# One TensorE program of attention and an FP4 feed-forward: Gram products in six pieces, the small chain's steps at other places, own matrices for the last batch, and a short end for three engines

## The chip, the core and the metric

The kernel runs on one core of one Trainium2 chip. The core has five engines with programs of their own: TensorE (PE; its weight loads are shown as PEld), VectorE (DVE), ScalarE (ACT), GpSimd (POOL) and SyncE (SP), which issues all DMAs here. They are tied by semaphores. The metric is the time of one execution in microseconds (us), the median of several runs. The profile comes from one profiled execution; its span starts when the first engine starts and ends with the last instruction.

## What is computed

`x` is (4, 2048, 256) float32: four batches of 2048 tokens. It is normalised row by row. Then two branches work on the result `xn`, and their product is added to `x`:

```python
xn = layernorm(x)
# attention, linear: no softmax, the norms run over the 2048 tokens
Q, K, V = xn @ Wq.T + bq, xn @ Wk.T + bk, xn @ Wv.T + bv
Q, K = l2_norm_over_tokens(Q), l2_norm_over_tokens(K)
tailor = 1.0 / (256 + einsum('bnc,bc->bn', Q.T, K.sum(-1) + 1e-6))
matrix = einsum('bmn,bcn->bmc', K, V)
s = xn + gamma * (V.sum(-1) + einsum('bnm,bmc->bcn', Q, matrix)) * tailor
# feed-forward, inputs and weights of each product rounded to blocks of FP4
h = silu(fp4(xn) @ fp4(w_gate).T) * (fp4(xn) @ fp4(w_up).T)      # 704 wide
g = silu(fp4(h) @ fp4(w_down).T)
out = x + s * g
```

## The kernel before

**Tiling.** The 8192 rows are taken in 32 pairs of 128-row tiles, 8 pairs to a batch. The kernel is one software pipeline over pairs, written once as `iteration(p, k, b, i)` for each engine and driven by `drive` (L290): iterations -1 to 11 written out, a hardware loop over batches 1 and 2 whose body is eight iterations, then iterations 28 to 32 written out, and a tail of iterations 33 to 43. In iteration p the input of pair p+3 is normalised and its scales found, pair p+1 is transposed, pair p goes through the gate and up products, pair p-1 is rounded to FP4, pair p-2 goes through the down product, pair p-10 through the attention product, and pair p-12 is added to `x` and stored. An iteration has two halves, j = 0 and 1 (one tile each), and each half two chunks c of 352 of the 704 hidden columns.

**The heavy work of an iteration.** On PE, for each chunk, `gate_up` (12 matmuls of 352 columns into `GU`), and with it a piece of the attention product of an older pair, `s_half` (6 matmuls of 128 columns, `GU<-Mx,xnT`); for each half the transposes of the rounded hidden values (`TR<-id,hq`, 11), those of the next inputs, and `down_product` (17 matmuls of 256 columns into `DS`). ACT makes `sil` from a gate chunk, copies transposes out of PSUM (`hqT`, `xqT`, `xnT`) and makes `gring` from `DS`. DVE multiplies `sil` with the up chunk (`h`, L840), finds the block scales (`ham`, `hss`, `hrr`), rounds (`ht`, L877, and `hg`, L880, which need `hT` of ACT, which needs `ht` of POOL, which needs `hrr`), scales (`hq`, four of 704), and makes `y` from the attention product and `gring` (`e_half`, `e_mul`). POOL divides by the scales and adds `y` and `x` (`o`, L527; L522 for the last seven pairs). `gate_up` may write a chunk once `h` of the chunk before last is done.

**The chain.** Q, K and V aren't formed. For each batch the products of the normalised rows with themselves, the Gram matrix, are summed over the 16 tiles of the batch in one PSUM bank `G` (L1389: 16 matmuls of 512 columns for its first block row, "gram0", and 16 of 384 for the second, "gram1"). From it a chain of small steps between PE (`ask`), ACT (`copy`), POOL (`inv`) and DVE (`answer`), all through the one bank `G`, makes the matrix `Mx` and a factor `unm` by which the rows of that batch are multiplied: turn, t1q, t1k, squares, norms, raw, tailor, product, top, high_low. The last, L974 to L980, writes `unm` and `Mx`, and `s_half` of the batch's first pair waits for it. Before it writes, DVE waits until `y` of all earlier batches is done, since there is one `Mx` and one `unm`.

**What sets the order.** Each engine runs its program in order. Where a chain step stands is a table with keys (i, j, slot): i is the iteration within the batch (i = p - 8b - 5), j the half, and slot 0, 1 or 2 a place in the half: on PE slot 0 is after the hidden transposes, slot 1 after the row transposes, slot 2 after the down product. ASKS is PE's table, ANSWERS DVE's, COPIES ACT's; the last batch has tables of its own (..._END), since its chain has no later iteration to spread into. For batches 0 to 2 the new matrices are first used at i = 5, j = 1. For the last batch this is iteration 34, in the tail, where PE only multiplies rows by `Mx` (`s_product`, 12 matmuls of 256 columns for a pair, into four places of `GU` in turn).

## Time and profile before

| | us |
|---|---|
| three runs | 630.25, 631.48, 631.04 (median 631.04) |
| the profiled execution, whole | 630.21 |
| its span | 628.4 |
| PE busy | 556.2 (89%) |
| DVE busy | 565.3 (90%) |
| ACT busy | 411.0 (65%) |
| POOL busy | 240.6 (38%) |

The profiled execution is 0.83 us under the median, and 1.8 us of it lie outside the span. The shares are means over stages in which different engines set the pace. PE's busy time is of pipelined matmuls whose ends are modelled, so a full PE row says that PE was never without work, not how fast it was. Where an engine waits, the row of the waiting instruction has the idle time and what ended it in brackets. A row by stretch has, behind the stretch and its length, the busy time and instruction count of PE, PEld, DVE, ACT and POOL, then the clock granted to TensorE (1.00 is 2.4 GHz, 0.50 is 1.2 GHz), the DMA share and GB/s.

### The profile page before, as it was taken

To read this page: it belongs to the slowest core of one execution; us is meant where nothing else is said; L and a number is where in the kernel's file an instruction comes from. 1 tells how busy PE (TensorE), PEld (TensorE's weight loads), DVE (VectorE), ACT (ScalarE), POOL (GpSimd) and SP (SyncE) were. 2 spreads that over 40 slices of the span, in tenths; PEclk is the share of its full clock that TensorE was granted. 3 is DMA by queue.
4 is the path that set the end of the run, shared out by engine and by line. 5 is a ranking of instruction groups with operands and counts; after the bars stand their busy time and mean duration, and the time that the engine had idled before them with its cause. 6 is when DMAs were issued, how large, how long until landed. Compare 5 with 4: busy or idle time off the path is not lost.

```text
span 628.4 us, 15141 instructions
## 1 busy us (share of the span) xinstructions
PE 556.2 (89%) x4957; PEld 427.8 (68%) x4957; DVE 565.3 (90%) x1201; ACT 411.0 (65%) x884; POOL 240.6 (38%) x208
## 2 busy tenths in 40 slices
PE   0276889999999999999999888999999999999667
PEld 0253667677787777678787665778888676788555
DVE  6979899999989999999899997999999999976824
ACT  3475788767678777667677775767777776555320
POOL 4443143443323344434443342443533344223316
PEclk9967899999999999999999999999999999999898
DMA  7010000000001001111101111111101111141213
GB/s 238 17 35 17 18 19 18 18 18 19 19 32 37 18 2 52 52 53 52 52 2 52 52 56 52 51 53 51 28 26 52 52 35 34 37 152 34 67 49 137
DMA packets 17473, 29.15 MB, mean 46 GB/s; under 512 B 2672, under 2 KB 4848, under 8 KB 17392
## 3 DMA queue, kind: packets, MB, share of 16 engines
q1 hardware_dynamic: 17392, 28.13, 13.7%
q8 instruction: 44, 0.72, 0.5%
q14 instruction: 37, 0.30, 0.2%
HBM read 19.73 MB, written 8.39 MB: 45 GB/s over the span
## 4 chain that ended last, share of the span: by engine, by line
PE 41%; DVE 34%; issue 15%; ACT 4%; POOL 2%; DVEq 2%; DMA 1%; POOLq 0%; SPq 0%; ACTq 0%
PE GU L1322 17%; PE DS L1332 5%; DVE hg L880 4%; DVE hq L888 4%; DVE h L840 4%; PE G L1389 4%; DVE ham L847 3%; PE DS L1334 3%; PE TR L1284 3%; DVE y L899 2%; DVE xq L829 2%; PE GU L1342 2%; DVE xt L820 2%; DVE st L794 1%; DVE xam L804 1%
## 5 line engine op out<-in xcount | busy, mean ns | idle before, releaser
L1322 PE MATMUL GU<-wgu,xqT 128*128 128x352 f16 x1536 | 255.8, 317 | 11.0 <-DVE h L840 4.3
L1322 PEld LDWEIGHTS GU<-wgu,xqT 128*128 128x128 f16 x1536 | 148.7, 100 | 88.4 <-issue 8.7
L592 ACT ACTIVATE sil<-GU,wkap 128x352 f32<-128x352 f32 x128 | 70.8, 553 | 71.6 <-PE GU L1322 70.5
L515 POOL TENSOR_TENSOR ht<-h,hrr 128x1408 f32<-128x1408 f32 x32 | 82.9, 2589 | 84.1 <-DVE hrr L854 82.5
L1332 PE MATMUL DS<-wdT,hqT 128*128 128x256 f16 x704 | 88.5, 275 | 2.6 <-ACT hqT L599 2.6
L840 DVE SCALAR_TENSOR_TENSOR h<-GU,wkap,sil 128x352 f32<-128x352 f32 x128 | 69.4, 542 | 18.8 <-ACT sil L592 15.6
L888 DVE TENSOR_TENSOR hq<-hg,hs 128x704 f16<-128x704 f16 x128 | 77.0, 642 | 1.0
L471 POOL TENSOR_TENSOR rs<-ve,half 128x2 f32<-128x2 f32 x32 | 25.2, 787 | 136.2 <-DVE ht L877 122.3
L481 POOL TENSOR_TENSOR xnat<-xs,xnat 128x510 f16<-128x510 f32 (+1 forms) x32 | 37.0, 1156 | 99.5 <-DVE hq L888 94.4
L1332 PEld LDWEIGHTS DS<-wdT,hqT 128*128 128x128 f16 x704 | 66.9, 99 | 11.7 <-ACT hqT L599 2.9
L1342 PE MATMUL GU<-Mx,xnT 128*128 128x128 f16 (+1 forms) x648 | 59.9, 233 | 5.2 <-DVE Mx L980 4.5
L1342 PEld LDWEIGHTS GU<-Mx,xnT 128*128 (+1 forms) x648 | 49.3, 99 | 17.6 <-issue 6.2
L628 ACT ACTIVATE gring<-DS,hun 128x256 f32<-128x256 f32 (+1 forms) x64 | 29.9, 467 | 43.6 <-issue 30.3
L599 ACT COPY hqT<-TR 128x768 f16<-128x768 f16 x64 | 51.0, 797 | 7.5 <-PE TR L1284 6.5
L877 DVE SCALAR_TENSOR_TENSOR ht<-hT,ht 128x1408 f32<-128x1408 f32 x32 | 51.8, 1618 | 3.5 <-ACT hT L641 3.4
L1284 PE MATMUL TR<-id,hq 128*128 128x128 f16 x704 | 49.7, 219 | 4.1 <-DVE hq L888 3.8
L1334 PE MATMUL DS<-wdT,hqT 128*128 128x256 f16 x384 | 52.6, 273 | 0.0
L880 DVE SCALAR_TENSOR_TENSOR hg<-hT,ht 128x1408 f16<-128x1408 f32 x32 | 51.7, 1616 | 0.0
L847 DVE TENSOR_REDUCE ham<-h 128x88 f32<-128x1408 f32 x32 | 51.4, 1607 | 0.0
L488 POOL TENSOR_TENSOR xt<-xs,xrr 128x512 f32<-128x512 f32 x32 | 34.1, 1066 | 36.1 <-DVE hq L888 28.4
L1284 PEld LDWEIGHTS TR<-id,hq 128*128 128x128 f16 x704 | 42.7, 98 | 6.8 <-DVE hq L888 5.1
L641 ACT ACTIVATE hT<-ht 128x1408 f32<-128x1408 f32 x32 | 43.9, 1371 | 2.8 <-POOL ht L515 2.2
(152 smaller groups left out, 932.7 us busy)
## 6 DMA issues: line engine op xcount, KB each, us to landing
xin<-in_L_attn_x SPq DMA_DIRECT2D x34, 256.0 KB, 2.9
xe<-in_L_attn_x SPq DMA_DIRECT2D x25, 256.0 KB, 2.8
out<-o SPq DMA_DIRECT2D x25, 256.0 KB, 2.1
algebra<-in_L_ffn_w_down SPq DMA_DIRECT2D x1, 704.0 KB, 6.4
gring<-in_L_ffn_w_gate SPq DMA_DIRECT2D x1, 640.0 KB, 4.6
gring<-in_L_ffn_w_up SPq DMA_DIRECT2D x1, 640.0 KB, 5.2
xs<-in_L_attn_x SPq DMA_DIRECT2D x2, 256.0 KB, 4.5
xt<-in_L_attn_x SPq DMA_DIRECT2D x2, 256.0 KB, 5.1
```

What stands on the lines that cost most here:

```text
L515: g.tensor_tensor(paired(ht[:, 0:2 * I]), paired(h[:, q]), spread(hrr[:, q], 4 * CB), ALU.mult).then_inc(S["ht_d"], 1)
L592: a.activation(sil[:, c], GU[:, c, 0, 0:CH], ACT.Silu, scale=wkap[:, 0:1]).then_inc(S["sil_d"], 1)
L840: v.scalar_tensor_tensor(h[:, k, (2 * j + c) * CH:(2 * j + c + 1) * CH], GU[:, c, 1, 0:CH], wkap[:, 0:1], sil[:, c], ALU.mult, ALU.mult).t ...
L847: v.tensor_reduce(per_block(ham[:, :]), paired_in_order(h[:, q]), AX.X, ALU.max, apply_absolute_value=True).then_inc(S["ham_d"], 1)
L877: v.scalar_tensor_tensor(ht[:, 0:2 * I], hT[:, 0:2 * I], CUT, ht[:, 0:2 * I], ALU.max, ALU.subtract).then_inc(S["hw_d"], 1)
L880: v.scalar_tensor_tensor(hg[:, 0:2 * I], hT[:, 0:2 * I], CUT, ht[:, 0:2 * I], ALU.max, ALU.subtract).then_inc(S["hg_d"], 1)
L888: v.tensor_tensor(paired(hq[:, q, j, at:at + I]), paired(hg[:, j * I:(j + 1) * I]), spread(scales[:, q, j * HB:(j + 1) * HB], HB), ALU.mul ...
L1284: last = t.transpose(TR[:, bank, zz * P:(zz + 1) * P], hq[:, q, j, z * P:(z + 1) * P], id16[:, :])
L1322: last = t.matmul(GU[:, c, m, 0:CH], xqT[:, k, j, 2 * a_ + kc], wgu[:, b_, kc, 2 * m + c], start=(z == 0 and kc == 0), stop=(z == 2 and kc ...
L1332: t.matmul(DS[:, 0:D], hqT[:, j, z], wdT[:, z], start=(z == 0), stop=False)
L1334: last = t.matmul(DS[:, 0:D], hqT[:, j, LOCH + z], wdT[:, NCH + z], start=False, stop=(z == LOCH))
L1342: last = t.matmul(bank, slot[:, j, 2 * a_ + kc], Mx[:, b_, kc, columns], start=(i == 0 and kc == 0), stop=(i == 2 and kc == KD - 1))
```

## The change

It has four parts.

- **Gram products in six pieces.** gram0 is now four asks of four tiles (it was two of eight), gram1 two of eight tiles (it was one of sixteen). The first piece of gram0 moves into the end of the batch before (i = 6), where it belongs to batch b + 1.
- **The chain's other steps for batches 0 to 2** move later by up to four slots, and `inv` on POOL moves from the end of i = 2 to i = 3. For the last batch high_low moves earlier: PE's transposes by one slot, DVE's part from the end of iteration 33 to the middle of 32.
- **Own matrices for the last batch.** `Mx_end` and a second column of `unm` are written and read by batch 3, and its high_low no longer waits for `y` of the earlier batches.
- **A short end.** Behind iteration 32, PE, ACT and DVE run a `tail()` of their own in place of iterations 33 to 43. SP and POOL keep theirs.

```diff
         ASKS = {(-3, 0, 2): "weights_q", (-3, 1, 2): "weights_k", (-2, 0, 2): "weights_v",
-                (-1, 1, 2): "gram0_first", (0, 0, 1): "gram0_last", (0, 1, 2): "gram1", (1, 0, 2): "turn", (1, 1, 2): "t1q",
-                (2, 0, 1): "t1k", (2, 1, 0): "norms", (2, 1, 2): "raw", (3, 0, 2): "tailor", (3, 1, 2): "product",
-                (4, 1, 0): "top", (5, 0, 0): "high_low"}
-        ANSWERS = {(-4, 1, 1): "own_basis", (0, 1, 0): "gram0", (1, 0, 1): "gram1", (1, 1, 0): "turn", (2, 0, 2): "squares",
-                   (2, 1, 1): "norms", (3, 1, 0): "tailor", (4, 0, 1): "product", (4, 1, 1): "top",
-                   (5, 0, 1): "high_low"}
+                (-2, 1, 2): "gram0_0", (-1, 0, 1): "gram0_1", (-1, 1, 1): "gram0_2", (6, 1, 2): "gram0_0", (0, 0, 1): "gram0_3",
+                (0, 1, 2): "gram1_0", (1, 0, 0): "gram1_1", (1, 0, 2): "turn", (2, 0, 0): "t1q", (2, 0, 2): "t1k",
+                (2, 1, 2): "norms", (3, 0, 2): "raw", (3, 1, 2): "tailor", (4, 0, 2): "product", (4, 1, 2): "top",
+                (5, 0, 1): "high_low"}
+        ANSWERS = {(-4, 1, 1): "own_basis", (0, 1, 0): "gram0", (1, 0, 1): "gram1", (1, 1, 0): "turn", (2, 1, 0): "squares",
+                   (3, 0, 0): "norms", (4, 0, 0): "tailor", (4, 1, 0): "product", (5, 0, 0): "top", (5, 0, 2): "high_low"}
...
-                    (3, 0, 2): "top", (3, 1, 1): "high_low"}
+                    (3, 0, 2): "top", (3, 1, 0): "high_low"}
...
-                       (2, 0, 1): "norms", (2, 1, 2): "tailor", (3, 0, 1): "product", (3, 1, 0): "top", (4, 1, 2): "high_low"}
+                       (2, 0, 1): "norms", (3, 0, 0): "tailor", (3, 0, 1): "product", (3, 0, 2): "top", (3, 0, 3): "high_low"}
...
-                    if step == "high_low":
+                    if step == "high_low" and not (isinstance(b, int) and b == BATCHES - 1):
 
                         wait(dve, "y_d", 4 * b * PB)
...
+            def tail():
+                for p in range(PAIRS + 1, PAIRS + LAGE):
+                    for j in range(2):
+                        e_mul(p, p % 2, j)
...
+            def tail():
+                last = BATCHES - 1
...
+                p, k, first = PAIRS + 1, (PAIRS + 1) % 2, PAIRS + 1 - LAGE
+                s_pair(first)
+                for c in range(2):
+                    hidden_transposes(p, k, 0, c, False)
+                s_pair(first + 1)
+                for c in range(2):
+                    hidden_transposes(p, k, 1, c, False)
+                down_product(p, k, 0)
+                s_pair(first + 2)
+                down_product(p, k, 1)
+                for e in range(first + 3, PAIRS):
+                    s_pair(e)
```

The two `tail()` shown are VectorE's and TensorE's. ScalarE's holds `hidden_out` and `g_out` for the two tiles of pair 31, one tile after the other. In COPIES, t1q moves from (2, 0, 0) to (2, 0, 1) and raw from (3, 0, 1) to (3, 1, 0). `hidden_out` is the two `hqT` copies of a tile, `g_out` its `gring`, and `s_pair(e)` the attention product of pair e; `first` is pair 23, and pairs from 24 on belong to the last batch.

**TensorE from iteration 32 to the end.** `G<-mtop,ones` is the ask of top, `G<-id,mt` that of high_low. Before:

```order
L1342 MATMUL GU<-Mx,xnT 128x256 x6
L1448 MATMUL G<-mtop,ones 128x1
L1284 MATMUL TR<-id,hq 128x128 x11
L1453 MATMUL G<-id,mt 128x128 x4
L1332 MATMUL DS<-wdT,hqT 128x256 x11
L1334 MATMUL DS<-wdT,hqT 128x256 x6
L1342 MATMUL GU<-Mx,xnT 128x256 x6
L1284 MATMUL TR<-id,hq 128x128 x11
L1332 MATMUL DS<-wdT,hqT 128x256 x11
L1334 MATMUL DS<-wdT,hqT 128x256 x6
...
L1342 MATMUL GU<-Mx,xnT 128x256 x102
```

After:

```order
L1478 MATMUL G<-id,mt 128x128 x4
L1354 MATMUL DS<-wdT,hqT 128x256 x11
L1356 MATMUL DS<-wdT,hqT 128x256 x6
L1365 MATMUL GU<-Mx,xnT 128x256 x18
L1306 MATMUL TR<-id,hq 128x128 x11
L1365 MATMUL GU<-Mx_end,xnT 128x256 x12
L1306 MATMUL TR<-id,hq 128x128 x11
L1354 MATMUL DS<-wdT,hqT 128x256 x11
L1356 MATMUL DS<-wdT,hqT 128x256 x6
L1365 MATMUL GU<-Mx_end,xnT 128x256 x12
L1354 MATMUL DS<-wdT,hqT 128x256 x11
L1356 MATMUL DS<-wdT,hqT 128x256 x6
```

Rows of the attention product now stand between the transposes of pair 31 and its down products, and 72 matmuls are left behind them instead of 96.

**VectorE over the same stretch**, from `y` of the first tile of pair 22 on (`ktop` to `kap` is top, `unm` to `Mx` is high_low). Before:

```order
L911 SCALAR_TENSOR_TENSOR y<-GU,unm,gring 128x256
L870 SCALAR_TENSOR_TENSOR hs<-hss,hbq,hs 128x44 x2
L877 SCALAR_TENSOR_TENSOR ht<-hT,ht 128x1408
L880 SCALAR_TENSOR_TENSOR hg<-hT,ht 128x1408
L969 COPY ktop<-G 128x1
L970 RECIPROCAL kap<-G 128x1
L972 TENSOR_SCALAR kap<-kap 128x1
L888 TENSOR_TENSOR hq<-hg,hs 128x704 x4
L911 SCALAR_TENSOR_TENSOR y<-GU,unm,gring 128x256 x3
L974 TENSOR_SCALAR unm<-ktop 128x1
L978 TENSOR_SCALAR Mx<-G,kap 128x512
L980 SCALAR_TENSOR_TENSOR Mx<-G,kap,Mx 128x512
```

After:

```order
L983 COPY ktop<-G 128x1
L984 RECIPROCAL kap<-G 128x1
L986 TENSOR_SCALAR kap<-kap 128x1
L884 SCALAR_TENSOR_TENSOR hs<-hss,hbq,hs 128x44 x2
L891 SCALAR_TENSOR_TENSOR ht<-hT,ht 128x1408
L990 TENSOR_SCALAR unm<-ktop 128x1
L994 TENSOR_SCALAR Mx_end<-G,kap 128x512
L996 SCALAR_TENSOR_TENSOR Mx_end<-G,kap,Mx_end 128x512
L894 SCALAR_TENSOR_TENSOR hg<-hT,ht 128x1408
L902 TENSOR_TENSOR hq<-hg,hs 128x704 x4
L925 SCALAR_TENSOR_TENSOR y<-GU,unm,gring 128x256 x19
```

Top moved ahead of `hs` and `ht`, high_low ahead of `hg`, and the other 19 `y` now stand in a row.

**VectorE in the loop, iteration i = 2 to 4** keeps its rows; squares (L931, L934) move behind `hg` of i = 2, norms to the start of i = 3, and tailor from behind `hg` of i = 3 to the start of i = 4.

## Rows read from the trace of the kernel before

**Rows 1.** Busy time by stretch: the last batch's first five iterations, and the end

```profile
511.10:583.60 72.50, 71.59 (x651) 55.62 (x648) 62.27 (x120) 40.81 (x81) 21.29 (x14) 1.00 0.17 56
583.60:628.40 44.80, 29.64 (x242) 24.46 (x241) 22.00 (x51) 9.34 (x17) 17.70 (x13) 0.86 0.25 89
```

**Rows 2.** DVE's waits in batch 1's chain, 270 to 330: total us, times, longest

```profile
DVE h L840 <- ACT sil L592: 2.2, 3, 0.9
DVE ht L877 <- ACT hT L641: 0.5, 1, 0.5
```

**Rows 3.** The same in batch 0's chain, 150 to 190

```profile
DVE h L840 <- ACT sil L592: 1.4, 3, 0.7
DVE ht L877 <- ACT hT L641: 0.8, 1, 0.8
```

**Rows 4.** Timeline of PE: gram1 of batch 1; first use of `Mx` of batch 1

```profile
265.27 3.61 PE L1389 MATMUL G<-xnat 128*128 x16 [1.18 <-DVE algebra L924]
...
346.74 0.70 PE L1342 MATMUL GU<-Mx,xnT 128*128 128x128 f16 x6 [0.92 <-DVE Mx L980]
```

**Rows 5.** Timeline of DVE in batch 1, i = 2, and at i = 5

```profile
290.83 0.58 DVE L840 SCALAR_TENSOR_TENSOR h<-GU,wkap,sil 128x352 f32<-128x352 f32 x1
...
292.18 1.27 DVE L931 TENSOR_TENSOR wqkv<-algebra,wqT 128x512 f32<-128x512 f32 x1
...
294.06 0.68 DVE L820 SCALAR_TENSOR_TENSOR xt<-xT,xt 128x512 f32<-128x512 f32 x1
...
297.72 0.48 DVE L840 SCALAR_TENSOR_TENSOR h<-GU,wkap,sil 128x352 f32<-128x352 f32 x1
...
351.19 0.48 DVE L840 SCALAR_TENSOR_TENSOR h<-GU,wkap,sil 128x352 f32<-128x352 f32 x1
```

**Rows 6.** Timeline of ACT: the `sil` of the three `h` of rows 5

```profile
290.05 0.57 ACT L592 ACTIVATE sil<-GU,wkap 128x352 f32<-128x352 f32 x1
...
296.19 0.55 ACT L592 ACTIVATE sil<-GU,wkap 128x352 f32<-128x352 f32 x1 [1.14 <-PE GU L1322]
...
347.52 0.54 ACT L592 ACTIVATE sil<-GU,wkap 128x352 f32<-128x352 f32 x1
```

**Rows 7.** Timeline of PE where the last batch begins

```profile
514.17 0.77 PE L1284 MATMUL TR<-id,hq 128*128 128x128 f16 x11 [0.79 <-DVE hq L888]
...
526.97 1.89 PE L1389 MATMUL G<-xnat 128*128 128x512 f16 x8
```

**Rows 8.** Timeline of all engines from the middle of iteration 32 on

```profile
590.26 0.48 DVE L911 SCALAR_TENSOR_TENSOR y<-GU,unm,gring 128x256 f32<-128x256 f32 x1 [1.76 <-POOL o L527]
...
595.07 1.83 DVE L888 TENSOR_TENSOR hq<-hg,hs 128x704 f16<-128x704 f16 x4
...
595.17 1.11 PE L1453 MATMUL G<-id,mt 128*128 128x128 f32 x4 [4.96 <-DVE kap L972]
...
606.65 1.36 PE L1332 MATMUL DS<-wdT,hqT 128*128 128x256 f16 x11 [1.31 <-ACT hqT L599]
...
608.75 0.47 ACT L628 ACTIVATE gring<-DS,hun 128x256 f32<-128x256 f32 x1 [2.20 <-issue]
...
610.01 0.75 DVE L978 TENSOR_SCALAR Mx<-G,kap 128x512 f16<-128x512 f32 x1
...
611.70 12.31 PE L1342 MATMUL GU<-Mx,xnT 128*128 128x256 f16 x96 [2.38 <-DVE Mx L980]
...
616.89 0.48 DVE L911 SCALAR_TENSOR_TENSOR y<-GU,unm,gring 128x256 f32<-128x256 f32 x1 [0.17 <-PE GU L1342]
617.54 0.48 DVE L911 SCALAR_TENSOR_TENSOR y<-GU,unm,gring 128x256 f32<-128x256 f32 x1 [0.17 <-PE GU L1342]
...
624.66 1.26 POOL L522 TENSOR_TENSOR xT<-y,xT 128x512 f32<-128x512 f32 x1
```

**Rows 9.** Stretches of the end at TensorE's lower clock

```profile
592.00:599.00 7.00, 3.83 (x19) 2.94 (x20) 4.83 (x9) 0.00 (x0) 0.00 (x0) 0.51 0.36 111
612.00:616.00 4.00, 4.00 (x24) 2.95 (x23) 1.45 (x3) 0.00 (x0) 1.27 (x1) 0.57 0.18 70
```

More of the change, by code:

```diff
@@ L173, in build @@
         kap = sb("kap", [P, 1])
-        unm = sb("unm", [P, 1])
+        unm = sb("unm", [P, 2])
         Mx = sb("Mx", [P, 2, KD, D], F16)
+        Mx_end = sb("Mx_end", [P, 2, KD, D], F16)
         xe = sb("xe", [P, 2, 2 * D])
@@ L516, in iteration @@
                                     ALU.mult).then_inc(S["ht_d"], 1)
+                last_batch = isinstance(b, int) and b == BATCHES - 1
+                if i == 3 and not last_batch:
+                    wait(pool, "nrm_d", b + 1)
+                    g.tensor_tensor(inv[:, :], nrm[:, :], half[:, :], ALU.pow).then_inc(S["inv_d"], 1)
                 if on["o"]:
@@ L973, in answer @@
                 if step == "high_low":
[L974 removed]
+                    z = int(isinstance(b, int) and b == BATCHES - 1)
+                    Mb = (Mx, Mx_end)[z]
+                    v.tensor_scalar(unm[:, z:z + 1], ktop[:, :], 1.0 / (MTOP * XSCALE), None, ALU.mult).then_inc(S["unm_d"], 1)
                     wait(dve, "kap_d", b + 1)
@@ L1203, in iteration @@
                     h_scales(p, k, 2)
-            drive(dve, iteration)
+            def tail():
+                for p in range(PAIRS + 1, PAIRS + LAGE):
+                    for j in range(2):
+                        e_mul(p, p % 2, j)
+            drive(dve, iteration, tail)
         @block.tensor
@@ L1338, in s_terms @@
                 slot = ring(xnT, e, TRING)
+                Mb = Mx_end if isinstance(e, int) and e >= PAIRS - PB else Mx
                 for i, (a_, b_) in enumerate(((1, 0), (0, 0), (0, 1))):
                     for kc in range(KD):
-                        last = t.matmul(bank, slot[:, j, 2 * a_ + kc], Mx[:, b_, kc, columns],
+                        last = t.matmul(bank, slot[:, j, 2 * a_ + kc], Mb[:, b_, kc, columns],
                                         start=(i == 0 and kc == 0), stop=(i == 2 and kc == KD - 1))
@@ L1376, in ask @@
                 tiles = TOKENS // P
-                if step in ("gram0_first", "gram0_last", "gram1"):
+                if step and step.startswith("gram"):
                     first = b * PB if isinstance(b, int) else own_value(pe, b * PB, PB, (BATCHES - 1) * PB)
-                    m = int(step == "gram1")
-                    n0, n1 = {"gram0_first": (0, PB), "gram0_last": (PB, tiles), "gram1": (0, tiles)}[step]
+                    m, part = int(step[4]), int(step[6])
+                    n0, n1 = part * tiles // (4 - 2 * m), (part + 1) * tiles // (4 - 2 * m)
                     wait(pe, "xlo", b * PB + n1 // 2)
                     wait(pe, "xhi", b * PB + n1 // 2)
-                    wait(pe, *(("gram_e2", 2 * b + 1) if m else ("mats", b)))
+                    if part == 0:
+                        wait(pe, *(("gram_e2", 2 * b + 1) if m else ("mats", b)))
                     if isinstance(b, int) and b == 0:
@@ L1499, in iteration, with tail, s_pair @@
                     attention(j, 2)
-            drive(pe, iteration)
+            def tail():
+                last = BATCHES - 1
+                def s_pair(e):
+                    p = e + LAGE
+                    for j in range(2):
+                        s_product(p, p % 2, j, last, e == PAIRS - PB and j == 0)
+                p, k, first = PAIRS + 1, (PAIRS + 1) % 2, PAIRS + 1 - LAGE
[10 more added lines that the diff above has]
+                    s_pair(e)
+            drive(pe, iteration, tail)
 _INS = ["L0_attn_x", "L0_attn_Wq", "L0_attn_bq", "L0_attn_Wk", "L0_attn_bk", "L0_attn_Wv", "L0_attn_bv",
```

81 lines of the change are left out of this document (43 added, 38 removed).

## The prediction, made before the changed kernel was run

> **What bounds the kernel now.** I read three things in turn: who is busy in which stretch, who waits for whom there, and the timeline around the waits. All times are of the profiled execution before; "earlier" is against them.
>
> In the long middle DVE sets the pace. Its waits are few: in batch 1's chain it waits three times for `sil` (2.2 us) and once for `hT` (0.5 us) [rows 2], in batch 0's for 1.4 and 0.8 us [rows 3]. Each wait for `sil` is PE arriving late with a chunk, because a chain step stands in front of it. So PE is the spare engine on average and the late one where chain steps crowd.
>
> From iteration 28 on PE sets it: busy 71.59 of 72.50 us, DVE 62.27 [rows 1]; its last wait there is 0.79 us at 514.17, for `hq` [rows 7].
>
> The end, 583.6 to 628.4, is set by neither: PE works 29.64 and DVE 22.00 of 44.80 us [rows 1]. It is a chain. PE stands 4.96 us in front of high_low's transposes, since DVE answers top only behind `ht` and `hg` (595.17). Then two rounds of transposes, copy by ACT and down product follow, with a wait of 1.31 us for the copy in each. Then DVE writes `Mx` at 610.01, because the one `Mx` can't be overwritten before the older `y` are done, and PE begins the last 96 attention matmuls after 2.38 us of waiting, at 611.70. The last POOL addition starts at 624.66 and ends at 625.92 [rows 8].
>
> **The end, after the change.** I walk it from the step that sets it.
>
> - Top is answered right behind `y` of pair 22's first tile, which ended at 590.74 [rows 8]; with three tiny operations, some 0.4 us in all, `kap` is there at 591.2. PE's four transposes, now one slot earlier, are done by about 592.3 at the 1.11 us that they took at the lower clock [rows 8]. Tailor's move behind `hss`, `hrr` and a `y` costs PE about 1 us in front of product; since that `y` waited 1.76 us for POOL before [rows 8], and POOL's division starts earlier by the same move, I take `y` as unmoved. Bounds: 0.4 us earlier to 0.8 later.
> - DVE does `ht`, then high_low: `unm` 0.15 and two of 0.75 us (the row at 610.01), 1.65 in all, then `hg` and `hq`. Before, the four `hq` ended at 596.90 [rows 8]; now at 598.55, the first two at 597.7. `Mx_end` is ready at about 595 instead of behind 611.
> - PE meanwhile does the down product, pair 22's second tile and pair 23, which no longer wait for anything, and then waits for `hq`. Transposes of tile 0 from 597.7, 0.7 us; pair 24's first tile 0.65; its second waits for `y` of pair 22, 599.05, and ends at 599.7. The price of a tile, 0.65 us, is the step from one `y` to the next at full clock (616.89 to 617.54) [rows 8].
> - Transposes of tile 1 wait for the copies of tile 0. Behind such transposes PE waited 1.31 us for the copies, so they run from 599.8 to 600.6. Down product of tile 0: 1.8 us (606.65 to the `gring` at 608.75 is 2.1, with the drain), to 602.4. Pair 25: 1.3, to 603.7. ACT has `gring` (0.47) and then tile 1's two copies (1.4), to 604.3: PE waits 0.7. Down product of tile 1 to 606.2.
> - Pairs 26 to 31: 12 tiles at 0.655, 7.9 us, to 614.1; `y` 0.5; POOL 1.26: 615.9 instead of 625.92. POOL isn't the bound: ten additions of 1.31 us from 599.1 end at 612.2.
>
> The end gives **10.0 us**. What covered what: the attention tiles that fill PE's waits for ACT cost nothing while ACT copies; without that cover they'd cost 0.65 each, 4 tiles, 2.6 us. SP and POOL keep their programs; SP's load of `x` for pair 24 is issued behind the store of pair 22, some 3 us before POOL needs it, which delays at most one addition that isn't on the path.
>
> **Gram in pieces, last batch.** gram0's first quarter, 0.87 us (half of the 1.89 that eight matmuls take from 526.97 on, less the drain of the last, some 0.15), moves to the end of iteration 27, in front of PE's 0.79 us wait at 514.17 [rows 7], and fills it. From there PE is never idle until iteration 32, so removing 0.87 behind and adding 0.1 in front gives **0.8 us**. Bounds: 0 (if DVE becomes the limit at once) and 0.87.
>
> **Batches 0 to 2.** PE's gram1 in batch 1 starts at 265.27, after 1.18 us of waiting for DVE's answer to gram0 [rows 4]. That answer isn't moved, so whatever PE saves ahead of it is lost in this wait. From there only half of its 3.61 us stands before the next chunk, which comes 1.7 us earlier, and DVE's longest wait, 0.9 us [rows 2], goes. The other half comes one chunk later; there PE is where it was and DVE 0.9 earlier than before: a new wait of about 0.1.
> Next `h` of i = 2: at 290.83 DVE was 0.21 behind `sil`, which ended at 290.62 [rows 5, 6]. With DVE 0.76 earlier it waits 0.55. Then squares, 1.9 us (292.18 to 294.06) [rows 5], no longer stand before the `h` at 297.72, while PE's t1q and t1k both still do. `sil` ended at 296.74, 0.98 before that `h` [rows 5, 6]; DVE would be there 2.1 earlier, and waits 1.0. That part of squares' time isn't lost work but a hole, since squares come afterwards. In i = 3 PE has norms, the shorter step, instead of raw in front, and the two other waits for `sil` go; raw's copy on ACT moves behind `hT`, so the 0.5 goes; about 0.3 appears at the second half. Before 2.7 us of waits, after 1.95: **0.7 us** for a batch, two batches 1.4. Batch 0, the same way: 2.2 before, 0.9 after: **1.3 us**. Bounds for the three: all waits go and none comes, 7.6 us; or the new holes come on top of half the old ones, minus 2 us. I take 2.7, between, from the rows.
> The end of the chain comes later. `Mx` was written 0.9 us late for PE at 346.74 [rows 4]; now, one slot later, 1.3 us more. The `h` behind it, at 351.19, was 3.1 us behind its `sil`, which ended at 348.06 [rows 5, 6]; that covers it. The first gram piece stands at the loop's end, where PE also leads.
>
> **Sum.** 630.2 - 10.0 - 0.8 - 2.7 = 616.7 for an execution like the profiled one, which was 0.8 under the median: **617.5 us**.
>
> **Rivals.**
> A. The clock. TensorE's granted clock was 0.51 in 592 to 599 and 0.57 in 612 to 616, near its level of 1.2 GHz instead of 2.4; ahead of the first lay PE's 4.96 us idle, ahead of the second idle times of 1.31, 1.31 and 2.38 us [rows 8, 9]. Now no wait over 1.5 us is left, but the small ones around 584 to 604 may still bring it down once: three tiles then cost double, 1.3 instead of 0.65, about 2 us. 619.5, chance 0.17.
> The Trainium skill ("TensorE: Matmul & The Clock Gate", HAM oscillation) says that idle gaps between bursts of matmuls return the array to half rate; the trace agrees before 595, and by that rule alone the end would keep its clock, with the 4.96 us gone.
> B. The middle gives nothing. t1q and t1k now stand in one half with squares behind; if the hole is 2 us in each of three batches, and the norms to product steps pass on theirs, the gain of 2.7 turns to a loss of 1 to 2: 620.2 to 622. Chance 0.18.
> C. The middle gives all its waits: 7.6 instead of 2.7, 612.6. Chance 0.12. For it: PE has slack on average. Against: the wait at 265.27 pins PE.
> D. The edit doesn't do what it says: the pieces are in a different place, but the end stays bound elsewhere, by `hq` or ACT's copies standing 3 us or more later than walked, 620.5 and above. Chance 0.05.
> E. Slower. The later chain holds PE at the first use of new matrices in each of batches 0 to 2. `Mx` would have to come more than 3 us of cover plus 4.5 (13.5 us of gain over three batches) later than it did; I found 1.3. Above 631. Chance 0.03.
>
> **Chances.** Forecast, 615.3 to 619: 0.45. A to D are all faster than before. The measurement tells about 0.2%, 1.3 us, from no change. The range takes in A and C and most of B: 612.3 to 621.8. Faster 0.96, same 0.01, slower 0.03.
>
> **What will show it.** Right: `Mx_end` written near 594 in these terms, no PE wait over 2 us behind it, the last 72 attention matmuls at a `y` every 0.65 us, the end some 10 us shorter from the last `ham` on. DVE's wait of 0.9 behind gram1 gone, new waits of 0.5 and 1.0 in the i = 2 of batches 1 and 2, the two of i = 3 gone. Wrong: a clock under 1.00 behind iteration 32; a PE wait at first use of `Mx` over 4 us; DVE waits in a batch above 2.7 us in sum.

## The result: 4 us faster, where 13.5 were forecast

| kernel | median | runs | ratio to before, 95% interval |
|---|---|---|---|
| before | 631.16 | 630.25 to 631.48 | |
| changed | 627.21 | 626.07 to 627.82 | 0.9938, 0.9919 to 0.9956 |

The forecast was 617.5 us in a range from 612.3 to 621.8. The changed kernel is 0.6% faster, clear of the interval, and outside the range. Its profiled execution took 627.52 us, with this page ahead of the rest (busy us, share of the span, instructions):

```profile
span 625.7 us, 15159 instructions
...
PE 557.6 (89%) x4957; PEld 431.0 (69%) x4957; DVE 576.7 (92%) x1201; ACT 409.8 (65%) x884; POOL 247.4 (40%) x208
```

PE's busy time has hardly moved, but DVE's has grown from 565.3 to 576.7 us with the same 1201 instructions. Some instruction on DVE takes longer than it did.

To find where, I cut the span at the ends of five `ham` (DVE's last scan of an iteration): those of iterations 3, 11, 19, 27 and 31. The last two columns are two experiments of the next section, tailor moved (e3_both) and gram0 answered sooner besides (e8_gram0_sooner).

| stretch, us | before | changed | forecast change | e3_both | e8_gram0_sooner |
|---|---|---|---|---|---|
| start to `ham` 3 | 108.70 | 109.25 | 0 | 108.46 | 110.02 |
| batch 0, 3 to 11 | 127.84 | 128.49 | -1.3 | 126.36 | 125.70 |
| batch 1, 11 to 19 | 138.55 | 141.84 | -0.7 | 139.40 | 136.42 |
| batch 2, 19 to 27 | 142.78 | 144.10 | -0.7 | 143.27 | 140.24 |
| last batch, 27 to 31 | 65.73 | 65.04 | -0.8 | 65.04 | 65.03 |
| end, behind `ham` 31 | 44.80 | 36.98 | -10.0 | 34.67 | 34.69 |
| span | 628.4 | 625.7 | -13.5 | 617.2 | 612.1 |

The end is 7.8 us shorter instead of 10.0. Batches 0 to 2 are 5.3 us longer in sum, where 2.7 less were forecast. Those two are 10.2 of the missing 10.8 us.

The stretch of the end as a row, with the columns of [rows 1]:

```profile
588.70:625.70 37.00, 26.35 (x243) 22.25 (x241) 24.16 (x51) 9.23 (x17) 17.67 (x13) 1.00 0.30 107
```

Against [rows 1] the granted clock is 1.00 instead of 0.86, so PE needs 3.3 us less for the same matmuls; but DVE is busy for 24.16 us instead of 22.00, with 51 instructions both times.

**The instruction that grew.** It stands in tailor, four tiny operations on a 128x2 tile. The view of one tile gives minimum, median and maximum in ns over the four batches; before the change:

```profile
L949 DVE TENSOR_SCALAR den<-den x4: 169/169/170, 183.1 to 583.7; 128x2 f32<-128x2 f32 x4
```

and in the changed kernel, the three that are in question:

```profile
L963 DVE TENSOR_SCALAR den<-den x4: 1933/2062/2474, 187.9 to 590.0; 128x2 f32<-128x2 f32 x4
L965 DVE RECIPROCAL den<-den x4: 165/166/166, 190.1 to 592.5; 128x2 f32<-128x2 f32 x4
L967 DVE TENSOR_SCALAR gt<-den,gam x4: 228/988/990, 190.3 to 592.7; 128x2 f32<-128x2 f32 x4
```

The addition of a constant to two columns takes 2.0 us instead of 0.17, and the product with `gam` 0.99 instead of 0.23 in three of four batches. Ahead of neither does the profile show idle time: the two microseconds are counted as the operation's own. The timeline of batch 1 tells what it stands beside, DVE first:

```profile
326.56 1.93 DVE L963 TENSOR_SCALAR den<-den 128x2 f32<-128x2 f32 x1
328.53 0.17 DVE L965 RECIPROCAL den<-den 128x2 f32<-128x2 f32 x1
328.73 0.99 DVE L967 TENSOR_SCALAR gt<-den,gam 128x2 f32<-128x2 f32 x1
```

and POOL:

```profile
325.88 2.59 POOL L520 TENSOR_TENSOR ht<-h,hrr 128x1408 f32<-128x1408 f32 x1 [1.45 <-DVE hrr L868]
328.43 1.26 POOL L536 TENSOR_TENSOR o<-y,xe 128x512 f32<-128x512 f32 x1
```

`den` ends at 328.49, 0.02 us behind the end of POOL's `ht` (328.47); `gt` at 329.72, 0.03 behind the end of POOL's `o`. The row of `ht` also tells why they meet: POOL starts it when DVE has `hrr`, and the change put tailor, two operations later, right behind `hrr`. Before, tailor stood where POOL was idle.

The Trainium skill ("SBUF — State Buffer", "Who interferes with whom") says that DVE and GpSimd share one pair of ports to SBUF, that `tensor_scalar` between SBUF tiles can take it, and that the loser is blocked for the whole of the other's instruction. The trace agrees to 0.03 us.

### The profile page after: what moved, and what is told of

It is laid out like the page before. It is cut to its first block and busy times, and to the rows that moved or that the text cites. A ratio compares the mean times of both kernels' runs of the same rounds, so it can differ in the third digit from the quotient of the medians.

```text
span 625.7 us, 15159 instructions
## 1 busy us (share of the span) xinstructions
PE 557.6 (89%) x4957; PEld 431.0 (69%) x4957; DVE 576.7 (92%) x1201; ACT 409.8 (65%) x884; POOL 247.4 (40%) x208
## 5 line engine op out<-in xcount | busy, mean ns | idle before, releaser
L1344 PE MATMUL GU<-wgu,xqT 128*128 128x352 f16 x1536 | 262.1, 323 | 7.3 <-DVE h L854 4.2
L1344 PEld LDWEIGHTS GU<-wgu,xqT 128*128 128x128 f16 x1536 | 151.5, 101 | 86.1 <-issue 5.0
L1354 PE MATMUL DS<-wdT,hqT 128*128 128x256 f16 x704 | 87.3, 272 | 1.1 <-ACT hqT L608 0.6
L902 DVE TENSOR_TENSOR hq<-hg,hs 128x704 f16<-128x704 f16 x128 | 78.3, 652 | 0.9
L1356 PE MATMUL DS<-wdT,hqT 128*128 128x256 f16 x384 | 52.4, 273 | 0.0
L1306 PE MATMUL TR<-id,hq 128*128 128x128 f16 x704 | 51.1, 222 | 0.9 <-DVE hq L902 0.9
L1365 PE MATMUL GU<-Mx,xnT 128*128 128x128 f16 (+1 forms) x552 | 48.0, 224 | 2.8 <-DVE y L913 2.8
L1365 PEld LDWEIGHTS GU<-Mx,xnT 128*128 (+1 forms) x552 | 40.0, 99 | 12.9 <-issue 3.0
L1306 PEld LDWEIGHTS TR<-id,hq 128*128 128x128 f16 x704 | 44.1, 100 | 3.5 <-DVE hq L902 1.1
L610 ACT COPY hqT<-TR 128x640 f16<-128x640 f16 x64 | 45.0, 703 | 0.0
```

Source lines behind the costliest of these rows:

```text
L902: v.tensor_tensor(paired(hq[:, q, j, at:at + I]), paired(hg[:, j * I:(j + 1) * I]), spread(scales[:, q, j * HB:(j + 1) * HB], HB), ALU.mul ...
L1306: last = t.transpose(TR[:, bank, zz * P:(zz + 1) * P], hq[:, q, j, z * P:(z + 1) * P], id16[:, :])
L1344: last = t.matmul(GU[:, c, m, 0:CH], xqT[:, k, j, 2 * a_ + kc], wgu[:, b_, kc, 2 * m + c], start=(z == 0 and kc == 0), stop=(z == 2 and kc ...
L1354: t.matmul(DS[:, 0:D], hqT[:, j, z], wdT[:, z], start=(z == 0), stop=False)
L1356: last = t.matmul(DS[:, 0:D], hqT[:, j, LOCH + z], wdT[:, NCH + z], start=False, stop=(z == LOCH))
L1365: last = t.matmul(bank, slot[:, j, 2 * a_ + kc], Mb[:, b_, kc, columns], start=(i == 0 and kc == 0), stop=(i == 2 and kc == KD - 1))
```

## The experiments

Each kernel is the changed one with the edit shown. "End" is the stretch behind `ham` 31. In the diffs, lines are cut short. The kernel before had a median of 630.37 us in the runs beside e1 to e4, 630.81 beside e5 to e8, 630.03 beside e9 to e12, and 630.53 beside e13. Where two medians lie closer than their intervals, the readings rest on the stretches and iterations of the profiled executions.

**e1_end_tailor**, the last batch's tailor back at its old place:

```diff
-                       (2, 0, 1): "norms", (3, 0, 0): "tailor", (3, 0, 1): "product",
+                       (2, 0, 1): "norms", (2, 1, 2): "tailor", (3, 0, 1): "product",
```

> The changed kernel with one move: in the last batch DVE answers tailor one slot sooner again, at (2, 1, 2), where it stood before the change, instead of behind hrr at (3, 0, 0). Theory, POOL holds DVE: in the changed kernel the operation den<-den (128x2) of the last batch took 2.47 us instead of 0.17 and ended with POOL's ht, and gt took 0.99 instead of 0.23. At the old place POOL is not in a long tensor_tensor, so den takes 0.17, product comes some 3 us earlier, and the end from the last ham on is 2 to 3 us shorter: 624.2 to 625.2 us. Rival, the operation waits for data of TensorE's tailor product: it stays long wherever it stands, 627. Rival, the end is bound by hq and ACT's copies: den is short and the end no shorter, 626.5 to 627.5.

Measured: 625.34 us, ratio 0.9923 (0.9904 to 0.9941). The `den` of the last batch takes 0.17 us again, and the end 34.67 us instead of 36.98. So 2.3 us of the end is the hold. The median is 1.9 us lower, just above what was expected, and its interval overlaps that of the changed kernel; it is the stretch that tells. The other three `den` are as long as before the edit.

**e2_loop_tailor**, the same for batches 0 to 2:

```diff
-                 (2, 1, 2): "norms", (3, 0, 2): "raw", (3, 1, 2): "tailor",
+                 (2, 1, 2): "norms", (3, 0, 2): "raw", (3, 1, 1): "tailor",
...
-                    (3, 0, 0): "norms", (4, 0, 0): "tailor", (4, 1, 0): "product",
+                    (3, 0, 0): "norms", (3, 1, 2): "tailor", (4, 1, 0): "product",
```

> The changed kernel with tailor moved in batches 0 to 2 alone: TensorE asks it at (3, 1, 1) instead of (3, 1, 2), and DVE answers it at (3, 1, 2) instead of at (4, 0, 0), which lies right behind hrr, with which POOL's ht starts. Theory, POOL holds DVE: den<-den takes 0.17 instead of 1.9 to 2.5 us and gt 0.23 instead of 0.99, the iteration i = 4 is some 2.5 to 3 us shorter in each of three batches: 618.5 to 620.5 us. Rival, the spread of the steps itself and the waits for mtop in front of top with the half clock behind them make the middle long: den is short, the iteration i = 5 or the wait for mtop grows by what is saved, 626 to 627. Rival, it waits for TensorE: den stays long, 627.

Measured: 622.48 us, ratio 0.988 (0.9864 to 0.9895). The three `den` of batches 0 to 2 take 0.17 us, and the iteration i = 4 takes 19.13 us instead of 21.18 in batches 1 and 2, and 17.42 instead of 19.55 in batch 0: 2.1 us for each, 6.2 in all, less than the 2.5 to 3 expected for each, and the median lies above the range expected.

**e3_both**, both edits:

> Both moves of tailor together, in the last batch and in batches 0 to 2. Theory, POOL holds DVE: the two gains add up, 615.5 to 618 us. If the gain of the last batch depends on how early its last full iteration ends (TensorE sets the pace there), the sum is short of it by up to 1 us, 619. Rivals as in the two single runs: 626 to 627.

Measured: 620.03 us, ratio 0.9839 (0.9825 to 0.9852). The two add up, but 1 to 2 us above what was expected. The end is now 34.67 us, 10.1 less than before the change; what is missing is all in batches 1 and 2 (the table above).

**e4_psum**, tailor left at the changed place, its first two operations made from PSUM:

```diff
-                    v.tensor_tensor(den[:, :], G[:, 0:2], inv[:, 0:2], ALU.mult).then_inc(S["cs_ev"], 1)
-                    wait(dve, "cs_ev", b + 1)
-                    v.tensor_scalar(den[:, :], den[:, :], float(D), None, ALU.add).then_inc(S["den1"], 1)
+                    v.tensor_scalar(den[:, 0:1], G[:, 0:1], inv[:, 0:1], float(D), ALU.mult, ALU.add).then_inc(S["den1"], 1)
+                    v.tensor_scalar(den[:, 1:2], G[:, 1:2], inv[:, 1:2], float(D), ALU.mult, ALU.add).then_inc(S["cs_ev"], 1)
+                    wait(dve, "cs_ev", b + 1)
```

> The changed kernel with tailor where the change put it, but den computed by two tensor_scalar operations from PSUM (G times inv, plus D) instead of a product from PSUM and an addition SBUF to SBUF in place. Theory, an operation of DVE with both ends in SBUF waits for POOL's running tensor_tensor: the two new operations take about 0.2 us each, but the reciprocal or the gt behind them, which reads SBUF, then meets the same POOL operation and is long instead, up to 2.4 us, and the time stays at 626 to 628. Rival, it is the addition alone that is slow (its in-place operand or its semaphore): no long operation is left and the middle gains 5 to 7 us, 620 to 622. Rival, any DVE operation at this place waits for something of TensorE: the first of the two PSUM operations is the long one, 627.

Measured: 626.79 us, ratio 0.9949 (0.9933 to 0.9964). DVE, and below it POOL, in batch 0:

```profile
187.61 0.21 DVE L961 TENSOR_SCALAR den<-G,inv 128x1 f32<-128x1 f32 x1
187.74 0.21 DVE L962 TENSOR_SCALAR den<-G,inv 128x1 f32<-128x1 f32 x1
187.98 0.17 DVE L965 RECIPROCAL den<-den 128x2 f32<-128x2 f32 x1
188.19 1.80 DVE L967 TENSOR_SCALAR gt<-den,gam 128x2 f32<-128x2 f32 x1
```

```profile
187.37 2.59 POOL L520 TENSOR_TENSOR ht<-h,hrr 128x1408 f32<-128x1408 f32 x1 [1.44 <-DVE hrr L868]
```

A `tensor_scalar` that reads PSUM isn't held, a `reciprocal` between SBUF tiles isn't held either, and the first `tensor_scalar` between SBUF tiles is, until POOL is done. The hold has only changed its carrier. TensorE's data are ruled out: the two operations that read them are the short ones. So is the wait for DVE's own semaphore, since the short `reciprocal` has one too.

**e11_extra_scalar and e12_extra_reciprocal** measure the hold by itself, on the fastest kernel (e8_gram0_sooner, below). In each of 31 iterations DVE does one operation more that nothing reads:

```diff
+        extra = sb("extra", [P, 32])
...
+                if on["m"] and on["mb"]:
+                    v.tensor_scalar(extra[:, 2 * (i + 6):2 * (i + 6) + 2], half[:, 0:2], 2.0, None, ALU.mult)
                 attention(0, 0)
```

> e8_gram0_sooner with one tensor_scalar more in each iteration from 1 to 31, 128x2 float32 SBUF to SBUF, which nothing reads, on DVE behind hrr and the first h and y, where POOL's ht (2.6 us) is running. It measures the hold by itself. Theory: each takes 1.6 to 2.0 us instead of 0.17 and ends with POOL's ht; some 24 of the 31 lie where DVE sets the pace, so the kernel takes 40 to 50 us longer than 613.5: 650 to 664 us. Rival, only tailor's operations are slow, for what they wait for: 0.17 each, 4 us, 617 to 618.

> The same as e11_extra_scalar with reciprocal in place of tensor_scalar, same tiles, sizes and places. In e4_psum a reciprocal between SBUF tiles took 0.17 us while POOL's ht ran, and the tensor_scalar behind it 1.7. Theory, the hold is on the kind of operation, not on SBUF as such: 0.17 us each, 24 of them 4 us, 616.5 to 618.5 us. Rival, any SBUF to SBUF operation at this place is held, and e4's reciprocal got by through its place: 650 us or more.

Measured: 659.35 us with the `tensor_scalar`, 612.38 with the `reciprocal`. One tile's row of each:

```profile
L1144 DVE TENSOR_SCALAR extra<-half x31: 690/2115/2377, 61.6 to 608.3; 128x2 f32<-128x2 f32 x31
```

```profile
L1144 DVE RECIPROCAL extra<-half x31: 152/154/157, 61.4 to 561.0; 128x2 f32<-128x2 f32 x31
```

Same tiles, same size, same place: 2.1 us against 0.15, and 47 us of the kernel's time. All 31 `tensor_scalar` end 0.02 to 0.03 us behind the POOL operation that they meet, 30 times `ht`, once `o`; all 31 `reciprocal` run through while the same POOL operations go on. The second kernel was expected to take 3 to 5 us more than e8_gram0_sooner, and its median is 1.1 us lower, with intervals that overlap; the last section tells where.

**e5 to e8: what the parts of the change are worth with tailor out of POOL's way.** e5_tail has the new end alone; e6_tail_pieces adds gram in six pieces, e7_tail_spread adds the later steps instead. The tables for batches 0 to 2 are otherwise those of the kernel before (and `inv` with them in e5 and e6), as in e6, here in part:

```diff
+                (2, 0, 1): "t1k", (2, 1, 0): "norms", (2, 1, 2): "raw", (3, 0, 2): "tailor", (3, 1, 2): "product",
+                (4, 1, 0): "top", (5, 0, 0): "high_low"}
```

> The end of the change alone: short programs of three engines behind the last full iteration, the own Mx_end and unm for the last batch, top and high_low answered in its last full iteration, tailor left at (2, 1, 2). Gram products in two pieces and all steps of batches 0 to 2 stand as in the kernel before. Theory: the end from the last ham on takes 34.7 us as with both moves of tailor, instead of 44.8, and nothing else moves: the kernel before less 10.1 us, 620.3, between 619.7 and 621. Rival, the end needs gram in pieces too (it brings PE 0.7 us sooner to the last full iteration, and the rest hangs on that): the end takes 35.5 or more. Rival, part of the gain is given back in batches: over 621.5.

> The end alone as in e5_tail, and besides the gram products in six pieces at the changed places, in all batches; the steps behind them (t1q to high_low, DVE's answers, ACT's copies, POOL's inv) stand in batches 0 to 2 as before. From the iterations of the run with both moves of tailor: pieces give 0.7 us in the last batch, and 0.86 in i = 1 of batches 1 and 2 each unless the wait of 2.5 us in front of gram1_0 is followed by the half clock, which costs 1.1 to 1.2 each. Theory, pieces gain and the half clock takes it back: 618.0 to 620.0 us, 618.9 in the middle, and the iterations i = 2 to 5 as in the kernel before. Rival, pieces gain nothing in the middle without the spread, since gram1_1 now stands in front of another chunk: 619.6 or more.

> The end alone as in e5_tail, and besides the spread of the steps from t1q to high_low in batches 0 to 2 with tailor clear of POOL's ht (asked at (3, 1, 1), answered at (3, 1, 2)); the gram products stay in two and one piece as before. From the iterations of the run with both moves of tailor: in batches 1 and 2, i = 2 is 0.84 us longer, i = 3 is 2.9 shorter, i = 4 is 2.15 longer and i = 5 is 0.4 longer, so 0.5 us lost in each; in batch 0, 1.4 us gained. Theory, the spread only moves the waits: 0.4 us gained in sum, 619.9 us, between 619.2 and 620.6. Rival, the spread is worth the 1 to 2 us that the waits for sil in i = 3 had, and the pieces spoil it: 618.5 or less.

| | median | ratio, 95% interval | batches 0, 1, 2 | last batch | end |
|---|---|---|---|---|---|
| before | 630.81 | | 127.84, 138.55, 142.78 | 65.73 | 44.80 |
| e5_tail | 620.40 | 0.9842, 0.9823 to 0.9861 | 127.85, 138.57, 142.70 | 65.73 | 34.66 |
| e6_tail_pieces | 619.28 | 0.9829, 0.9811 to 0.9847 | 127.74, 137.76, 142.96 | 65.04 | 34.68 |
| e7_tail_spread | 619.45 | 0.982, 0.9806 to 0.9835 | 126.56, 138.66, 142.49 | 65.75 | 34.67 |

The end is worth 10.1 us by itself and hangs on nothing else. The pieces give 0.69 us in the last batch and 0.86 in i = 1 of batch 1 (17.44 instead of 18.30); in batch 2 that iteration took 18.67, with a wait of 2.10 us ahead of gram1_0 and TensorE's clock down behind it. The spread gives 1.3 us in batch 0 and nothing in 1 and 2: i = 3 is 2.9 us shorter, and i = 2, 4 and 5 are 0.4, 2.15 and 0.4 longer. The medians of e5 to e7 lie 1.1 us apart with overlapping intervals; the split rests on the iterations, which repeat from kernel to kernel within 0.07 us where the clock is the same, but for the one at the loop's jump (i = 7 of batch 1, 20.2 to 20.6 us).

**e8_gram0_sooner**: e3_both with DVE's answer to gram0 one slot sooner.

```diff
-        ANSWERS = {(-4, 1, 1): "own_basis", (0, 1, 0): "gram0",
+        ANSWERS = {(-4, 1, 1): "own_basis", (0, 0, 2): "gram0",
```

> The changed kernel with both moves of tailor, and besides DVE's answer to gram0 in batches 0 to 2 one slot sooner, at (0, 0, 2) instead of (0, 1, 0). Theory: the wait of PE in front of gram1_0 (0.76, 2.55 and 2.1 us in the run without this move) goes or falls under 1 us, no half clock follows behind it, and i = 1 of batches 1 and 2 takes 17.4 us instead of 18.6: 1.5 to 2.5 us faster than with both moves of tailor, 617.5 to 618.7. Rival, DVE is the bound there and the wait costs nothing: no wait of PE is left and the time is 619.5 to 620.3 all the same. Rival, the half clock comes without the wait: i = 1 stays at 18.6.

Measured: **613.49 us, ratio 0.9723 (0.9708 to 0.9737)**, 6.5 us under e3_both and 4 us better than the best expected. PE's row at gram1_0 of batch 1, first in e3_both, then here, where no wait is left:

```profile
263.55 2.73 PE L1414 MATMUL G<-xnat 128*128 x8 [2.55 <-DVE algebra L938]
```

```profile
261.74 1.46 PE L1404 MATMUL G<-xnat 128*128 x8
```

DVE's waits in the changed kernel, 270 to 347 (total us, times, longest), came to the same 2.2 us as in [rows 2]:

```profile
DVE h L854 <- ACT sil L601: 2.2, 4, 0.7
```

In e8_gram0_sooner the same view of 250 to 357 has no row at all. In batch 1, against e3_both, i = 0 is 0.46 us shorter, i = 1 is 1.56 and i = 2 is 0.97. Of the 1.56, 1.2 is what the fallen clock behind the wait cost e3_both (last section), and 0.36 what the wait costs at full clock. The 0.97 is the hole for `sil` that the prediction had seen coming (0.32 and 0.75 us at `h`): with PE 2.5 us earlier, it doesn't open. Most of it is the second, 0.75: where the wait of 0.32 is gone, `xt` behind it is held for longer, 1.28 us instead of 0.97, and ends no sooner in the iteration. The 0.46 I had not thought of. It is another hold: in e3_both DVE's `xt`, which reads two SBUF tiles, meets POOL's `o`:

```profile
255.34 1.28 DVE L834 SCALAR_TENSOR_TENSOR xt<-xT,xt 128x512 f32<-128x512 f32 x1
```

```profile
254.79 1.27 POOL L536 TENSOR_TENSOR o<-y,xe 128x512 f32<-128x512 f32 x1
```

In e8_gram0_sooner gram0's answer, which reads PSUM, stands in front of it until POOL's `o` is done, at 256.96:

```profile
256.24 0.41 DVE L924 TENSOR_SCALAR algebra<-G 128x256 f32<-128x256 f32 x1
256.69 0.42 DVE L928 SCALAR_TENSOR_TENSOR algebra<-G,algebra 128x256 f32<-128x256 f32 x1
257.03 0.68 DVE L824 SCALAR_TENSOR_TENSOR xt<-xT,xt 128x512 f32<-128x512 f32 x1
```

**e9_gram0_pieces**, e6_tail_pieces with the same one-slot move: what is the spread worth once PE isn't held?

> As e6_tail_pieces (the end, and gram in six pieces, the steps from t1q on in batches 0 to 2 as in the kernel before), and besides DVE's answer to gram0 at (0, 0, 2). With e8_gram0_sooner, which has the spread besides, it tells what the spread is worth once PE no longer waits in front of gram1_0. Theory, spread and wait share the gain: in batches 1 and 2 the iterations i = 2 to 5 took 70.9 us with the old steps and 70.5 with the spread, in batch 0 66.6 and 64.5, so the old steps cost 0.4, 0.4 and 2.1 us, 616.4 us, between 615 and 617.5. Rival, the waits for sil in i = 3 (2.9 us longer there than with the spread) came of the wait in front of gram1 alone, PE arriving late ever since: they go here too, and the time is that of e8_gram0_sooner or less, 612 to 614. Rival, gram0's answer gains only with the spread: 618.5 or more.

Measured: 615.85 us, ratio 0.9776 (0.976 to 0.9793). Batches 0, 1 and 2 took 127.84, 136.86 and 140.71 us, against 125.70, 136.42 and 140.24 with the spread. The old steps still have i = 3 at 19.46 us: its waits don't come of gram1. The spread is worth 2.1 us in batch 0 and 0.45 in each of the others.

**e10_gram0_only**, the changed kernel as it is with that one move:

> The changed kernel with one entry different: DVE's answer to gram0 at (0, 0, 2) in batches 0 to 2; tailor is left where the change put it, behind hrr in all batches. Theory, the two causes are independent: POOL's hold on tailor still costs 2.1 us in each of batches 0 to 2 and 2.3 in the last, on top of e8_gram0_sooner's 613.5, so 621.5 to 622.5. Rival, with PE ahead the hold is absorbed by slack that the sooner answer makes: 617 to 619. Rival, the hold makes PE late again and hides the gain of the sooner answer: 624 or more.

Measured: 621.78 us, ratio 0.986 (0.9841 to 0.988). The iteration i = 4 is back at 21.17 us and the end at 36.98. The hold and the wait ahead of gram1 are separate costs, and they add.

**e13_inv_behind_o.** One thing was left: in batches 1 and 2 the spread takes 1.8 us of waits for `sil` out of i = 3, and i = 3 to 5 together are only 0.3 us shorter. In e8_gram0_sooner DVE's two steps `xt` and `xg` of i = 3, and POOL beside them:

```profile
307.06 0.68 DVE L824 SCALAR_TENSOR_TENSOR xt<-xT,xt 128x512 f32<-128x512 f32 x1
307.78 1.64 DVE L827 SCALAR_TENSOR_TENSOR xg<-xT,xt 128x512 f16<-128x512 f32 x1
```

```profile
306.50 1.01 POOL L515 TENSOR_TENSOR inv<-nrm,half 128x4 f32<-128x4 f32 x1
307.48 1.39 POOL L526 TENSOR_TENSOR o<-y,xe 128x512 f32<-128x512 f32 x1
```

The change put `inv` between `ht` and `o`; `o` runs 1 us later and meets `xg`. Moving `inv` behind `o`:

```diff
-                if i == 3 and not last_batch:
-                    wait(pool, "nrm_d", b + 1)
-                    g.tensor_tensor(inv[:, :], nrm[:, :], half[:, :], ALU.pow).then_inc(S["inv_d"], 1)
                 if on["o"]:
...
                         g.tensor_tensor(o[:, ko], y[:, ko], xe[:, ko], ALU.add).then_inc(S["o_d"], 1)
+                if i == 3 and not last_batch:
+                    wait(pool, "nrm_d", b + 1)
+                    g.tensor_tensor(inv[:, :], nrm[:, :], half[:, :], ALU.pow).then_inc(S["inv_d"], 1)
```

> e8_gram0_sooner with POOL's inv of batches 0 to 2 behind the addition o of i = 3 instead of between ht and o, where the change put it (before the change it stood at the end of i = 2). In e8's trace inv (1.01 us) pushes o to 307.48 to 308.87, and DVE's xg, two SBUF inputs, takes 1.64 us instead of 0.69 at 307.78. Theory: the work of DVE that grew where the spread took waits away is holds by POOL. With inv behind o, o runs from 306.5 to 307.8; xg takes 0.69, but xt in front of it is then held for some 0.6, so that i = 3 of batches 1 and 2 takes 16.2 instead of 16.58 us, and the kernel 0.7 to 1.2 us less than e8_gram0_sooner's 613.5: 612.3 to 612.9, with the clock at the loop's jump (1.7 us, at full or half) as the uncertainty. Rival, xg is long for another reason (its f16 output, ACT's xT): it stays at 1.64 us, i = 3 at 16.58. Rival, POOL comes late with inv and tailor waits for it: a DVE wait at den.

Measured: **612.28 us, ratio 0.971 (0.9697 to 0.9724)**, the fastest of all, though its interval overlaps that of e8_gram0_sooner. What it tells is in the iterations: i = 3 takes 16.21 and 16.22 us instead of 16.58 and 16.57, as worked out, and `xg` its 0.69 us, with `xt` now the one that is held:

```profile
306.27 1.27 DVE L824 SCALAR_TENSOR_TENSOR xt<-xT,xt 128x512 f32<-128x512 f32 x1
307.57 0.69 DVE L827 SCALAR_TENSOR_TENSOR xg<-xT,xt 128x512 f16<-128x512 f32 x1
```

## Why the prediction was wrong, step by step

- **The end.** The step that failed is "Tailor's move behind `hss`, `hrr` and a `y` costs PE about 1 us in front of product; ... I take `y` as unmoved". I counted tailor's operations at what they had taken before, and wrote in the same sentence that POOL's division starts earlier, without asking what DVE does beside it. The hold put product, `kap` and all behind it 2.3 us later, outside the bounds of 0.4 earlier to 0.8 later. PE's wait of 2.78 us for `y` at 596.95 is that lateness. With tailor moved (e1, e3) the end measures 34.7 us, 10.1 less, where the walk from step to step gave 10.0. The last 72 matmuls took 8.02 us, with a `y` each 0.65 us; forecast were 7.9. The load of `x` for pair 24 did come late, by 2.08 us, and off the path.
- **The last batch.** 0.69 us against 0.8. Right: the kernels with pieces in it take 65.0 there, those without 65.7.
- **Batch 0.** 1.3 forecast; 0.65 lost in the changed kernel, 1.5 gained with tailor clear of POOL. Right, but for the hold of 2.1, which I had costed at nothing: in the middle I named tailor's new place and gave it no price.
- **Batches 1 and 2.** 0.7 forecast for each. With tailor clear (e3) they are 0.85 and 0.5 us slower than before. The waits behaved as told: 0.9 at gram1 gone (i = 1 at 17.43 us where TensorE kept its clock), new ones of 0.32 and 0.75 against 0.55 and 1.0 forecast, those of i = 3 gone. Two things ate the gain. The waits gone from i = 3 came back as holds: `xg` of i = 3 takes 1.64 us instead of 0.69 since `inv` pushes `o` (e13), and `xt` of i = 4 takes 1.28 instead of 0.68 beside the next `o`, 1.55 us together of the 1.8 that the waits had been. The failed step there is that the sum counts waits alone and leaves every operation of DVE at the duration that it had; `inv`'s move on POOL, which was given no price, is 0.36 us of it in each batch (e13). Batch 0, where POOL has no `o` yet, is the control: none of these operations is held there, and the spread gives what was forecast. And the wait at gram1 that I said "pins PE" grew to 2.1 to 2.5 us, behind which TensorE's clock fell in both batches of e3, 1.2 us each. That cost too is in part a hold: `h` waits 0.3 us more for `sil`, and DVE's `copy` in gram1's answer, now later, meets POOL's `o` and takes 1.30 and 1.26 us instead of 0.56. In the changed kernel the clock fell there in batch 1 alone and cost 1.6 us, which is the larger part of why batch 1 lost 3.3 us and batch 2 1.3.
- **The rivals.** B, the middle turning to a loss of 1 to 2 us, is the direction that came (5.3 us lost); its reason (the hole of 2 us in i = 2) was not: the measured holes are 1.07. C, all waits gone, had against it the wait at 265.27 that pins PE. That was the right lever. It takes one entry of a table to move it (e8), and then no wait is left and batches 0 to 2 gain 2.1, 2.1 and 2.5 us. A, the clock in the end, did not come: 1.00 throughout, at waits up to 2.78 us; the clock fell in the middle, for which the range had no term of its own. D, the end bound elsewhere, came at 2.3 us, by an operation that it doesn't name. E did not come.
- **The range** had no term for an operation that takes ten times as long at another place. A sign stood in rows that I had quoted: squares' 128x512 product took 1.27 us at 292.18 [rows 5], where the kernels with the spread show 0.69 for it, and batch 0 of the kernel before itself 0.68. I read 1.27 as its price.

## What to carry to other kernels

The duration of a DVE operation between SBUF tiles is no constant: before moving one, look on POOL's timeline at what will run at the new place, above all right behind the operation that releases POOL. If one kind of tile operation shows two durations in a profile (0.68 and 1.28 us), find what runs beside the long one before using either as a price. And where a step "pins" an engine, moving that step by one slot is the first experiment: here it was worth more than either of the two rearrangements around it. Each move on the engine at the other side of the hold (`inv` on POOL) needs the same look.

The largest hold of this kernel was there before the change, and none of the runs touches it. DVE's first two `hq` of an iteration release POOL's `xnat`, and the third `hq` runs into it. In e8_gram0_sooner, DVE and POOL:

```profile
263.67 0.96 DVE L892 TENSOR_TENSOR hq<-hg,hs 128x704 f16<-128x704 f16 x2
265.30 1.62 DVE L892 TENSOR_TENSOR hq<-hg,hs 128x704 f16<-128x704 f16 x2
```

```profile
264.95 1.16 POOL L476 TENSOR_TENSOR xnat<-xs,xnat 128x510 f32 x1 [3.13 <-DVE hq L892]
```

The third takes up to 1.2 us instead of 0.52 (the second row has it together with the fourth), in 27 of 32 iterations, all that have POOL's `xnat` beside them. That is 16.2 us of DVE's time in the kernel before and 17.5 here. That POOL is the cause follows from the ends of the two operations, as with the other holds; what moving one of them would give isn't measured.
